# GpSimd makes every product with C in the middle batches of a bidirectional Mamba and expert kernel; sums of even and odd expert tiles go to two accumulators

## The reference, cut to what matters

```python
# block 1, for each batch, in both directions over the 512 tokens (l), 256 channels (d), 16 states (n)
dA  = exp(delta[d, l] * A[d, n]);  dBx = delta[d, l] * B[n, l] * u[d, l]
h[l] = dA[l] * h[l-1] + dBx[l]                  # the scan
y[d, l] = sum_n h[d, l, n] * C[n, l] + D[d] * u[d, l]
out1 = (y_forward + y_backward) * silu(z) @ out_proj
# block 2: each token goes to its 4 best of 16 experts, with weights w (softmax over the 4)
out2 = sum_k w[k] * (gelu(xn @ w1[e_k] + b1[e_k]) @ w2[e_k] + b2[e_k])
return x + out1 + out2
```

## Time and profile before

| what | value |
|---|---|
| median of 3 runs | 1144.69 us (1136.71 to 1153.21) |
| profiled execution, time and span | 1141.97 us, 1140.1 us |
| DVE busy | 1042.6 us, 91% |
| ACT busy | 940.7 us, 83% |
| PE busy | 933.3 us, 82%, mean granted clock 0.938 |
| POOL busy | 900.5 us, 79% |
| POOL's products L783 | 237, 510.1 us busy |
| POOL's sends L768 | 160 issues, 252.5 us busy, 61.1 us idle before them |
| DVE's products L1487 | 19, 36.4 us busy |

### The profile page before, as it was taken

One profiled execution on the slowest core, in us unless ns is written; L12 is line 12 of the kernel. 1 busy time (PEld: TensorE's weight loads), 2 busy tenths in 40 slices (PEclk: granted clock), 3 DMA queues, 4 the chain that ended last, 5 costly groups with the idle time before them and its releaser, 6 DMA issues.

```text
span 1140.1 us, 21850 instructions
## 1 busy us (share of the span) xinstructions
PE 933.3 (82%) x5866; PEld 738.2 (65%) x5866; DVE 1042.6 (91%) x1354; ACT 940.7 (83%) x1732; POOL 900.5 (79%) x545
## 2 busy tenths in 40 slices
PE   4476886754899988999998889899999989898982
PEld 2233332323678777878877677788788778776771
DVE  7878998959999999999999999999999999896991
ACT  4258888775899999999998889999999999887920
POOL 3278778657579979998999799799989989995742
PEclk9789989775899999999999999999999999998995
DMA  9924564486666867687687668677866877764545
GB/s 312 365 102 166 203 220 183 158 327 191 231 177 167 215 196 186 180 233 193 174 218 187 181 175 238 184 184 194 224 188 172 220 202 203 170 158 124 140 111 159
DMA packets 151299, 222.65 MB, mean 195 GB/s; under 512 B 36028, under 2 KB 97756, under 8 KB 146276
## 3 DMA queue, kind: packets, MB, share of 16 engines
q1 hardware_dynamic: 124036, 202.16, 56.0%
q0 software_dynamic: 27136, 19.02, 11.7%
HBM read 159.74 MB, written 65.52 MB: 198 GB/s over the span
## 4 chain that ended last, share of the span: by engine, by line
issue 22%; POOL 17%; DMA 6%; PE 6%; ACT 5%; DVE 3%; SPq 2%; POOLq 0%; DVEq 0%; ACTq 0%
POOL arena L783 9%; POOL acc_d L768 8%; DMA acc_d<-yrows,tags 4%; DVE arena L1479 2%; PE ps L1188 2%; ACT arena L990 2%; DMA tags<-slots_d 1%; PE ps L1159 1%; DVE ps L1467 1%; PE ps L1220 1%; ACT arena L930 1%; ACT arena L911 1%; ACT arena L958 1%; PE ps L1180 1%; DMA arena<-acc_d 0%
## 5 line engine op out<-in xcount | busy, mean ns | idle before, releaser
L1479 DVE TENSOR_TENSOR_SCAN arena<-arena,ps 128x512 f32<-128x512 f32 x512 | 597.3, 1201 | 1.1 <-issue 1.0
L783 POOL TENSOR_TENSOR arena<-arena 128x1024 f32<-128x1024 f32 x237 | 510.1, 2455 | 68.2 <-DVE arena L1479 67.4
L990 ACT ACTIVATE arena<-delta,a_neg 128x511 f32<-128x511 f32 x512 | 340.5, 726 | 6.0 <-DVE arena L1426 3.3
L768 POOL DMA_INDIRECT acc_d<-yrows,tags x160 | 252.5, 1578 | 61.1 <-issue 36.4
L1159 PE MATMUL ps<-ident,arena 128*128 128x128 f32 x2048 | 274.1, 278 | 7.5 <-POOL arena L783 5.1
L1467 DVE TENSOR_TENSOR ps<-du,ps 128x512 f32<-128x512 f32 x352 | 232.3, 675 | 23.0 <-PE ps L1223 20.4
L1159 PEld LDWEIGHTS ps<-ident,arena 128*128 128x128 f32 x2048 | 236.4, 144 | 20.7 <-POOL arena L783 5.6
L750 POOL DMA_INDIRECT slots_d<-arena,pos x128 | 161.0, 1258 | 47.3 <-issue 44.4
L1188 PE MATMUL ps<-w,arena 128*128 128x128 f32 x1248 | 174.7, 283 | 3.5 <-ACT arena L958 2.4
L1180 PE MATMUL ps<-rowsT,w 128*128 128x256 f32 x640 | 155.8, 387 | 11.6 <-ACT arena L941 7.6
L1188 PEld LDWEIGHTS ps<-w,arena 128*128 128x128 f32 x1248 | 154.2, 192 | 14.0 <-issue 4.5
(11 more groups left out here) (147 smaller groups left out, 913.5 us busy)
## 6 DMA issues: line engine op xcount, KB each, us to landing
arena<-c_d SPq DMA_DIRECT2D x128, 512.0 KB, 4.2
w<-w_dram SPq DMA_DIRECT2D x80, 258.0 KB
w<-w_dram SPq DMA_DIRECT2D x80, 256.0 KB
rows<-slots_d SPq DMA_DIRECT2D x80, 130.0 KB
slots_d<-delta SPq DMA_DIRECT2D x5, 2015.0 KB, 19.2
delta_d<-arena SPq DMA_DIRECT2D x8, 1024.0 KB, 3.9
du_d<-delta SPq DMA_DIRECT2D x8, 1024.0 KB, 6.2
delta<-delta_d SPq DMA_DIRECT2D x8, 1024.0 KB, 7.4
```

What stands on the lines that cost most here:

```text
L768: pool.indirect_dma_start(acc_d, bass.IndirectOffsetOnAxis(ap=tags[:, j, a, 0:1].bitcast(I32), axis=0), yrows[:, j % W_RING, a, :], None, ...
L783: nc.gpsimd.tensor_tensor(state[:, q % H_RING], state[:, q % H_RING], c_rows[:, r % C_RING], ALU.mult).then_inc(s["prod_done"], 1)
L990: nc.scalar.activation(decay[:, q % DA_RING, j, lo:lo + L - 1], delta[:, par, dh, lo:lo + L - 1], ACT.Exp, scale=a_neg[:, dh, 2 * g + j:2 ...
L1479: nc.vector.tensor_tensor_scan(state[:, q % H_RING, j, way], decay[:, q % DA_RING, j, way], b_ps[:, ROW[q, j], j, way], 0.0, ALU.mult, ALU ...
```

## The change

`VECTOR`, the table of the pairs whose product DVE makes in batches 1 to 6, becomes empty; the tables of batches 0 and 7 stay. In the same kernel `acc_d` becomes two tensors. Even tiles are added to the first, which is filled with `x` as before, odd tiles to the second. POOL zeroes half of `du` with a memset and SP writes it to the second one in 4 DMAs of up to 1 MB. A send waits for the tile before the last (the same accumulator) in place of the last. At the end SP reads both back (16 pieces), and DVE makes 16 additions in place of 8. The second accumulator's landing place in SBUF is that of the hidden activations.

```diff
-VECTOR = (16,)
+VECTOR = ()
...
+ZERO_ROWS = DH * L // D
+ZERO_ACC = [(at, min(ZERO_ROWS, (UNUSED + TOK - at) // P)) for at in range(0, UNUSED + TOK, P * ZERO_ROWS)]
+ACC_DMAS = 1 + BATCH + len(ZERO_ACC)
...
-        acc_d = dram("acc_d", (UNUSED + TOK, D))
+        acc_d = [dram(f"acc{i}_d", (UNUSED + TOK, D)) for i in range(W_RING)]
...
-        acc = decay.rearrange("p r j l -> p (r j l)")[:, 0:BATCH * TPB * D].rearrange("p (b n) -> p b n", b=BATCH)
+        acc = [t[:, 0:BATCH * TPB * D].rearrange("p (b n) -> p b n", b=BATCH)
+               for t in (decay.rearrange("p r j l -> p (r j l)"), hidden_all)]
...
             store_gate(0)
             store_gate(1)
+            sp.wait_ge(s["zero_acc"], 1)
+            for at, n in ZERO_ACC:
+                sp.dma_start(acc_d[1][at:at + P * n].rearrange("(p r) d -> p (r d)", p=P),
+                             du[:, 0, :, :].rearrange("p q l -> p (q l)")[:, 0:n * D]).then_inc(s["acc_filled"], 16)
...
             for i in range(W_RING):
                 sp.wait_ge(y_out[i], 16 * SH * (NTILE // W_RING))
+                for b in range(BATCH):
+                    sp.dma_start(acc[i][:, b, :], acc_d[i][UNUSED + L * b:UNUSED + L * (b + 1)].rearrange("(p t) d -> p (t d)", p=P))\
+                        .then_inc(acc_in[i][b], 16)
             for b in range(BATCH):
-                sp.dma_start(acc[:, b, :], acc_d[UNUSED + L * b:UNUSED + L * (b + 1)].rearrange("(p t) d -> p (t d)", p=P))\
-                    .then_inc(acc_in[b], 16)
-            for b in range(BATCH):
-                sp.wait_ge(s["acc_ready"], b + 1)
+                sp.wait_ge(s["acc_ready"], BATCH + b)
...
+            nc.gpsimd.memset(du[:, 0, :, :], 0.0).then_inc(s["zero_acc"], 1)
...
                 half = MPB // W_RING * (b - before)
-                for i in range(W_RING):
-                    wait(pool, y_out[i], 16 * SH * (half + (j + W_RING - 1 - i) // W_RING))
-                    pool.sem_inc(s["pool_step"], 1)
+                wait(pool, y_out[j % W_RING], 16 * SH * (half + j // W_RING))
+                pool.sem_inc(s["pool_step"], 1)
...
-                    pool.indirect_dma_start(acc_d, bass.IndirectOffsetOnAxis(ap=tags[:, j, a, 0:1].bitcast(I32), axis=0),
+                    pool.indirect_dma_start(acc_d[j % W_RING], bass.IndirectOffsetOnAxis(ap=tags[:, j, a, 0:1].bitcast(I32), axis=0),
...
+            for b in range(BATCH - 1):
+                dve.wait_ge(acc_in[0][b], 16)
+                nc.vector.tensor_tensor(acc[0][:, b, :], acc[0][:, b, :], scanned[b * 2 // BATCH][:, b % (BATCH // 2), :],
+                                        ALU.add).then_inc(s["acc_ready"], 1)
             for b in range(BATCH):
-                dve.wait_ge(acc_in[b], 16)
+                dve.wait_ge(acc_in[1][b], 16)
...
+            bank_written(dve, s, BATCH, "O", 0, 1, True)
+            dve.wait_ge(s["acc_last"], 1)
+            nc.vector.tensor_tensor(acc[0][:, BATCH - 1, :], acc[0][:, BATCH - 1, :], m_ps[1], ALU.add).then_inc(s["acc_ready"], 1)
```

More of the change, by code:

```diff
@@ L369, in build_kernel @@
         late = delta[:, 0].rearrange("p q l -> p (q l)").rearrange("p (t f s) -> p t f s", t=2, f=FC)
-        hidden = carve(GROUP * FC * S).rearrange("p (t f s) -> p t f s", t=GROUP, f=FC)
+        hidden_all = carve(GROUP * FC * S)
+        hidden = hidden_all.rearrange("p (t f s) -> p t f s", t=GROUP, f=FC)
         hidden = [hidden[:, t] for t in range(GROUP)] + [late[:, t] for t in range(2)]
-        acc = decay.rearrange("p r j l -> p (r j l)")[:, 0:BATCH * TPB * D].rearrange("p (b n) -> p b n", b=BATCH)
+        acc = [t[:, 0:BATCH * TPB * D].rearrange("p (b n) -> p b n", b=BATCH)
+               for t in (decay.rearrange("p r j l -> p (r j l)"), hidden_all)]
         scanned = [t[:, 0, :, :].rearrange("p q l -> p (q l)").rearrange("p (b n) -> p b n", b=BATCH // 2) for t in (delta, du)]
@@ L451, in build_kernel @@
         m_ps = [ps[:, 6, :], ps[:, 7, :]]
-        names = """consts_in route_in wts_in a_exp zero_v slots_zeroed var_ready std_ready xn_ready xnT_ps xnT_ready
+        names = """consts_in route_in wts_in a_exp zero_v zero_acc slots_zeroed var_ready std_ready xn_ready xnT_ps xnT_ready
             kw_ready bias_ready behind_ready experts_ready xn_act_ready shift_ready score_ps score_ready sel_ready logit_ps keys_ps chosen_ready rank_ps pos_ready gdiff_ready gexp_ready
@@ L462, in build_kernel @@
             b2_in b2_split b2_out turn_ps turned scaled
-            mixed_out mixed_in sp_step pool_step acc_ready out_done"""
+            mixed_out mixed_in sp_step pool_step acc_ready acc_last out_done"""
         s = {n: sem(n) for n in names.split()}
@@ L470, in build_kernel @@
         y_out = [sem(f"y_out{i}") for i in range(W_RING)]
-        acc_in = [sem(f"acc_in{b}") for b in range(BATCH)]
+        acc_in = [[sem(f"acc{i}_in{b}") for b in range(BATCH)] for i in range(W_RING)]
         block = ctx.enter_context(nc.Block())
@@ L510, in _ @@
                              delta[:, :, :, :].rearrange("p a q l -> p (a q l)")[:, 0:n * RW]).then_inc(s["slots_zeroed"], 16)
-            sp.dma_start(acc_d[0:UNUSED], x_in[0:UNUSED]).then_inc(s["acc_filled"], 16)
+            sp.dma_start(acc_d[0][0:UNUSED], x_in[0:UNUSED]).then_inc(s["acc_filled"], 16)
             for b in range(BATCH):
-                sp.dma_start(acc_d[UNUSED + L * b:UNUSED + L * (b + 1)].rearrange("(p t) d -> p t d", p=P),
+                sp.dma_start(acc_d[0][UNUSED + L * b:UNUSED + L * (b + 1)].rearrange("(p t) d -> p t d", p=P),
                              x_in[L * b:L * (b + 1)].rearrange("(t p) d -> p t d", p=P)).then_inc(s["acc_filled"], 16)
@@ L561, in read_ahead @@
                 sp.wait_ge(s["slots_zeroed"], 16 * ZERO_DMAS)
+                sp.wait_ge(s["acc_filled"], 16 * ACC_DMAS)
                 for k in range(3):
@@ L751, in _ @@
                         ap=pos[:, t * TOPK + k:t * TOPK + k + 1], axis=0), xn[:, t, :], None).then_inc(s["scattered"], 16)
-            pool.wait_ge(s["acc_filled"], 16 + 16 * BATCH)
+            pool.wait_ge(s["acc_filled"], 16 * ACC_DMAS)
             pool.wait_ge(s["prepared"], 1)
```

9 lines of the change are left out of this document (4 added, 5 removed).

## The result

The changed kernel takes 1125.54 us in the median (four runs, 1122.8 to 1127.85); the kernel before took 1140.7 us beside it (four, 1135.42 to 1153.21). The ratio is 0.9874, 95% interval [0.984, 0.9908]: faster by 1.3%, and the interval leaves out 1, but it is less than the 2% that the prediction took as the line. The profiled execution took 1122.8 us where that of before took 1141.97, so 19.2 us less; its span is 1121.0 us. The forecast for it was 1118.2. Against the kernel before beside it the medians differ by 15.2 us, where the prediction added up 23.8.

The account below looks back on a forecast made before the run. DVE's own work was taken to bound the middle, a chain of sends and landings the end. Savings of 15.3 + 9 - 0.5 = 23.8 us gave 1118.2 for the profiled execution, 1120.9 against the median, stated as 1120; range 1109 to 1137.

Parts of the forecast that it names:

- Part 1: Batches 1 to 6: six products leave DVE, all 15.3 us on the path, DVE's need falling from 616.5 to 601.2 us.
- rival A: The middle gives nothing, as POOL's lag or the shared port takes back DVE's saving: 1136 us; chance 0.2.
- Part 2: Batches 1 to 6: six more products on POOL still fit, its need 596.4 to 598.8 us against DVE's 601.2.
- C: Slower: POOL becomes the bound of the middle batches and stays it, for instance 1173 us; chance 0.05.
- Part 3: The end: two accumulators let sends go without waiting for the last tile's landing; 9 us gained, bounds 6.4 to 12.4.
- rival D: Tiles 8 and 9 still strung one behind the other by PSUM banks, so about 1130 us; chance 0.03.
- the walk: Tiles 6 to 9 at the end, send and landing times estimated in turn; last landing 1109.6 to 1116.2, against 1124.76.
- Part 4: The preparation: POOL's memset and 4.1 MB of zeros written cost 0.5 us, bounds 0 and 10.

Follow-up runs that it names:

- half_pool: The changed kernel with every product of POOL cut to half its width; 1123.24 us, ratio 0.9876 to the kernel before.
- mixed_out: The changed kernel with the two transfers that bring the scan's part back at the end cut from 1.75 MB to 0.5 MB; 1125.54 us, ratio 0.9867 to before.
- vector_21: The changed kernel with the product of pair 21 back on DVE in each middle batch; 1139.03 us, ratio 0.9971 to the kernel before.
- acc_alone: The changed kernel with the product of pair 16 kept on DVE, so two accumulators without the moved products; 1132.85 us, ratio 0.9965 to the kernel before.
- changed: The changed kernel, unaltered, run once more beside the follow-up kernels; 1123.17 us, ratio 0.9864 to the kernel before.
- after: The changed kernel as first measured and profiled, nothing altered; 1125.54 us, ratio 0.9874 to the kernel before.

## Why the prediction was right, and where not

The sum said 1118.2 us for the profiled execution; it took 1122.8. Forecast 1120 us, measured 1125.54. That the miss is under 6 us is in part luck. Middle and end brought 7.7 us less than forecast, but the preparation came out 1.8 us better and batch 7 1.2 us, the latter at a granted clock of 0.96 against 0.94. The median of the kernel before was also 4 us lower in the comparison than in the runs that the prediction started from.

**Part 1 was mis-sized, and it is the step that failed.** "Nothing lies beside them (no idle before them), so all 15.3 us are on the path" gives a saving that did not come: in the profiled executions it was 9.2 us. DVE's busy time in the middle fell by 13.5 us (608.52 to 595.02), and its idle time grew by 4.3. Idle time of zero before an instruction says that it delays DVE, not that DVE won't wait later for what the delay had hidden. The trace of before had the numbers: the fill ended 0.52 us before DVE needed it, and its batches 2 and 5, with a clean product, took 100.77 and 100.64 us, where 99.5 to 100.5 was to come without one. The stretched part, on the other hand, was real: a long product costs the batch about its excess over 1.2 us. Over the three executions with a product at pair 16, 8 of 18 were above 3 us; in each of the eight POOL began a product between 0.33 us before DVE's start and 0.57 us after it, in the ten others 0.72 us or more after it. The prediction told the clean ones by a send that POOL was issuing; but POOL was issuing one at 417.39 too (from 416.67, its timeline). What parts the two is when its next product began.

Of DVE's instructions in the middle the stretch hit the one with both operands in SBUF. L1478, with one operand in PSUM, took 677 ns in the mean beside 192 products of POOL, and 675 beside 186. The Trainium skill (SBUF — State Buffer, Who interferes with whom) says that a DVE instruction with two SBUF inputs contends with a GpSimd instruction that reads SBUF, and one with at most one such input, outside the 2-port modes, doesn't; the trace agrees with it on which instruction suffers. The Trainium skill's rule that moving work between these two engines "might not help" (Perfetto Trace Analysis, Optimizing Scalar/DVE Operations), rival A here, did not decide: the move ended the contention, since nothing on DVE was left that could contend.

**Part 2 was right.** POOL carried 192 products and 120 half-tile sends at the forecast price; its wait for DVE fell to 9.7 us (under 15 forecast), PE's for rows to 3.6, and half_pool shows that POOL's load costs the middle nothing. Periods were 100.4 to 101.5 and one 103.6, where 99.5 to 100.5 was forecast. Rivals A and C fell with it.

**Part 3 was right in mechanism, 1.6 us too high, within its bounds of 6.4 to 12.4.** POOL's landing waits are gone, and tiles 7 and 8 were sent 3.8 and 3.9 us after the one before (rival D is out); tile 9 came 7.2 us after tile 8, where 3.7 to 4.5 was forecast, since ACT waited 6.59 us for tile 7's landing. The term that was too small is the landing: 7.65 us for tile 7 and 6.76 us for tile 9, each of which the walk gave 3.4 to 7.4. The first comes from the reads of the scan's part, as mixed_out shows; the prediction knew of these reads, but not which tiles they would lie beside. The second lay beside the first eight reads of an accumulator, which the prediction called hidden behind tile 9: their time is hidden, their weight on tile 9's landing is not. In mixed_out, sent ahead of them, tile 9 landed in 3.3 us; no run changed these reads alone. Only part of what mixed_out gave the send (3.1 us) reached the end (2.3), since DVE's additions, with 2.4 us of waits among them, and SP's 16 reads, which start behind the last scan (1106.33), then set most of it.

**Part 4:** the 4.1 MB of zeros show no cost. At the same granted clock of 0.87 the first gate starts at 371.7 us against 373.0, and the first product of POOL at 268.97 instead of 270.66.

## What to carry to other kernels

Before you book the removal of an instruction from the busiest engine, look downstream in the same period: for each wait that the engine would meet sooner, compare when its operand is ready with when it is used now, and book only the slack. A mean over a mixture (1.2 and 4 us) hides that its two kinds have different worth, so count them apart. Where an order is static, moving one copy ahead of a table load was worth 0.65 us in four of six batches, where taking a whole clean operation off the bound engine was worth 0.06 or less.

## What the runs showed of the hardware that was not expected

- Which of the two engines is held doesn't go by who starts first. In the earlier trace rows DVE's product began 0.28 us before POOL's and took 3.97 us instead of 1.22; POOL's took 2.60, as others right after a send. When POOL began 0.72 us or more after DVE, nothing was stretched. In all eight stretched products at pair 16, and in the six of vector_21, DVE's product ended 1.09 us (within 0.01) after POOL's, whether it had started 1.69 us after POOL's or 0.57 us ahead. So nearly all of it was done only when POOL's was over. Why a head start of 0.57 us is worth nothing stays open. The two extremes (timelines of DVE and POOL, acc_alone, then vector_21):

```profile
527.30 4.25 DVE L1498 TENSOR_TENSOR arena<-arena 128x1024 f32<-128x1024 f32 x1
527.86 2.59 POOL L794 TENSOR_TENSOR arena<-arena 128x1024 f32<-128x1024 f32 x1
```

```profile
440.93 2.00 DVE L1498 TENSOR_TENSOR arena<-arena 128x1024 f32<-128x1024 f32 x1
439.25 2.58 POOL L794 TENSOR_TENSOR arena<-arena 128x1024 f32<-128x1024 f32 x1
```

- The landing of an accumulating send went from at most 3.7 us (mixed_out, tile 7: second issue at 1097.02, ACT not waiting for it at 1100.75) to 7.65 us beside 1.75 MB of plain reads, and for tile 9 from 3.3 (mixed_out) to 6.7 or 6.8 us (changed, after) beside eight reads of 256 KB.
- The preparation's time goes with the granted clock: 371.7 to 373.0 us in the three executions at 0.87, 376.0 to 381.1 in the eleven at 0.81 to 0.83. Batch 7's goes with it in the same way (table of stages); whether the clock makes the batch longer, or the waits in it lower the clock, is not shown.
- Open: batch 3 took 102.1 to 105.3 us in kernels that don't differ there, with DVE waiting for PE's fills and, in half_pool, 2.9 us of PE for which the profile names no cause.
